# Graph-network kernel: the third mean pass scans in PSUM, and counting marks are spread more densely over the sort

## What is computed

```python
def _sage_conv(x, src, dst, Wl, bl, Wr):
    msg = x[src]
    summed = segment_sum(msg, dst, num_segments=N_NODES)
    cnt = segment_sum(ones, dst, num_segments=N_NODES)
    mean = summed / maximum(cnt, 1.0)[:, None]
    return mean @ Wl.T + bl + x @ Wr.T

h = relu(_sage_conv(x, src, dst, Wl0, bl0, Wr0))
h = relu(_sage_conv(h, src, dst, Wl1, bl1, Wr1))
h = _sage_conv(h, src, dst, Wl2, bl2, Wr2)
x = layernorm(x + h)
```

## Time and profile before

| | |
|---|---|
| median of 3 runs | 2670.53 us |
| the profiled execution | 2668.62 us, of which its span, first to last instruction, is 2666.8 us |
| TensorE (PE) busy | 1858.4 us, 70% |
| VectorE (DVE) busy | 1730.9 us, 65% |
| ScalarE (ACT) busy | 1097.3 us, 41% |
| GpSimd (POOL) busy | 1772.3 us, 66% |
| mean granted TensorE clock | 0.852 of full |

### The profile page before, as it was taken

The page is one execution under the profiler, slowest core; times in us unless marked ns, Lnnn a source line. Parts: engine busy times, 40 slices in busy tenths (PEclk is TensorE's granted clock), DMA queues, the critical chain, the costliest instruction groups (busy, mean ns, idle before and its releaser), DMA issues.

```text
span 2666.8 us, 43662 instructions
## 1 busy us (share of the span) xinstructions
PE 1858.4 (70%) x10441; PEld 1326.4 (50%) x10441; DVE 1730.9 (65%) x5671; ACT 1097.3 (41%) x2508; POOL 1772.3 (66%) x1895
## 2 busy tenths in 40 slices
PE   4536666999979999687777764888778888770000
PEld 2425555666656666465555543555555555540000
DVE  7766977677757777665555543798888887881000
ACT  6952110445434444222222222676666666650000
POOL 0045775776637676447777777777777777776776
PEclk6667999999989999788888786899999999995555
DMA  0014665988969988454444522555444454433231
GB/s 19 0 52 112 170 154 139 179 194 187 191 141 176 192 200 187 131 144 120 138 128 139 160 87 85 148 152 156 146 148 144 143 157 138 147 110 103 93 94 50
DMA packets 366725, 356.94 MB, mean 134 GB/s; under 512 B 46535, under 2 KB 288725, under 8 KB 366585
## 3 DMA queue, kind: packets, MB, share of 16 engines
q1 hardware_dynamic: 310136, 246.40, 30.6%
q0 software_dynamic: 56448, 109.10, 21.5%
HBM read 232.83 MB, written 129.11 MB: 136 GB/s over the span
## 4 chain that ended last, share of the span: by engine, by line
PE 33%; POOL 25%; DVE 17%; issue 17%; DMA 5%; ACT 2%; POOLq 1%; DVEq 0%; SPq 0%; ACTq 0%
POOL GX L674 11%; POOL hsrc L674 8%; PE bank L851 8%; PE bank L871 5%; POOL out_dram L728 4%; PE bank L773 4%; PE bank L899 3%; PE bank L891 3%; PE bank L889 3%; DMA GX<-in_x_dram,idx_a 2%; PE bank L855 2%; DVE hsrc L1231 2%; DVE stats L1357 2%; POOL x_prime L728 2%; DVE hsrc L1232 2%
## 5 line engine op out<-in xcount | busy, mean ns | idle before, releaser
L674 POOL DMA_INDIRECT GX<-mean_product,idx_a x392 | 412.4, 1052 | 128.0 <-issue 114.1
L674 POOL DMA_INDIRECT GX<-in_x_dram,idx_a x392 | 377.8, 964 | 118.3 <-issue 111.1
L851 PE MATMUL bank<-h,wt 128*128 128x512 f32 x588 | 316.3, 649 | 0.0
L1045 ACT ACTIVATE logv<-mv,eps 128x4 f32<-128x4 f32 x245 | 72.2, 295 | 545.9 <-DVE mv L1362 545.8
L728 POOL DMA_INDIRECT x_prime<-normed,idx_b x196 | 198.4, 1012 | 95.9 <-issue 91.7
L728 POOL DMA_INDIRECT out_dram<-XN,idx_b x196 | 192.7, 983 | 74.3 <-issue 64.6
L674 POOL DMA_INDIRECT hsrc<-x_prime,idx_d x196 | 189.1, 965 | 59.7 <-issue 59.7
L674 POOL DMA_INDIRECT GX<-in_edge_attr_dram,idx_a x196 | 189.2, 965 | 58.6 <-issue 53.5
L674 POOL DMA_INDIRECT hsrc<-x_prime,idx_c x196 | 186.6, 952 | 59.7 <-issue 59.7
L773 PE MATMUL bank<-ident,GX 128*128 128x128 f32 x588 | 107.2, 313 | 152.8 <-DMA GX<-in_x_dram,idx_a 146.6
L773 PE MATMUL bank<-ident,hsrc 128*128 128x128 f32 x468 | 86.1, 315 | 157.8 <-DMA hsrc<-x_prime,idx_d 58.2
(11 more groups left out here) (231 smaller groups left out, 4658.5 us busy)
## 6 DMA issues: line engine op xcount, KB each, us to landing
mean_product<-prod SPq DMA_DIRECT2D x147, 256.0 KB
hsrc<-mean_product SPq DMA_DIRECT2D x147, 256.0 KB, 4.4
XN<-in_x_dram SPq DMA_DIRECT2D x98, 256.0 KB, 5.9
x_prime<-normed SPq DMA_DIRECT2D x98, 256.0 KB
XN<-x_prime SPq DMA_DIRECT2D x98, 256.0 KB, 4.6
out_dram<-normed SPq DMA_DIRECT2D x98, 256.0 KB
flag<-same_dst_row SPq DMA_DIRECT2D x147, 128.0 KB, 4.7
XN<-low_row SPq DMA_DIRECT2D x98, 128.0 KB
```

The source lines that it names most:

```text
L674: pool.indirect_dma_start(buf[:, c.slot(U), t, :], None, table, bass.IndirectOffsetOnAxis(ap=idx[:, c.slot(U), t:t + 1], axis=0)).then_inc ...
L851: last = pe.matmul(psum[:, :], wt[:, T_R[i], :], before[:, c.slot(2), :], start=True, stop=not dst_phase)
```

## The change

There are two edits. First, in `mean2` (i = 2) ScalarE rectifies bank 5 in place, VectorE scans straight from bank 5, nothing is written to `hsrc`, and TensorE waits before it writes bank 5 not only until ScalarE is through (`m_h`) but also until the scan of the chunk before is (`m_seg`). Second, the counts of marks: 50 for 44 at the start, 14 for 12 behind an even turn, 3 for 2 in the formula behind an odd one.

```diff
-            mark(44)
+            mark(50)
@@
-                mark(12 if turns % 2 == 0 else 2 + turns // 2)
+                mark(14 if turns % 2 == 0 else 3 + turns // 2)
@@ def mean_turn(c):
                     pe.wait_ge(m_h.of(c), m_h.after(c, 1))
+                    if c.phase == "mean2":
+                        pe.wait_ge(m_seg.of(c), m_seg.after(c, 1))
                     psum = bank[5]
@@ def mean_keep(c):
-                    act.activation(h, bank[5][:, :], ACT.Relu, bias=bcol[:, i - 1:i]).then_inc(m_h.of(c), 1)
+                    act.activation(h if i == 1 else bank[5][:, :], bank[5][:, :], ACT.Relu, bias=bcol[:, i - 1:i]).then_inc(m_h.of(c), 1)
@@ def mean_seg(c):
-                    rows = take_cols(hsrc, c.index() * CH, CH)
+                    rows = take_cols(hsrc, c.index() * CH, CH) if c.phase == "mean1" else bank[5][:, :]
```

## The result

The changed kernel takes 2656.05 us (median of 6 runs, 2651.78 to 2658.71), the kernel before 2670.53 (6 runs, 2667.63 to 2672.39): a ratio of 0.9947, 95% interval [0.9934, 0.9959], so 14.5 us or 0.53% faster.

A forecast was written before the change was run, and what follows sets the result against it. ScalarE's marks bound the tail before mean0, POOL's gathers mean0's middle, TensorE the later mean passes. Gain 16.6 us (16.1 plus 0.5), less 0.7 for bank 5, is 15.9: 2654.6 us against 2670.53, range 2651 to 2660.

The forecast's parts named there:

- Cost in the sort: At the start, TensorE waits for ScalarE's marks before turns 9, 11, 13 and the value columns, turned 4.1 us late.
- Gain in the tail: Behind the value turns fewer marks remain, so mean0's first GX turn comes at 192.05, 16.1 us earlier.
- The clock: In mean0's prologue TensorE's higher clock comes sooner: 0.5 us gained, of a possible 1.4.
- POOL: In mean0's gathers, the first stop shrinks from 22.7 to 2.5 us, the second stays 5.2, and 16.1 us passes through.
- a second stop that grows: Sign of a wrong forecast: POOL's second stop in mean0's gathers, expected near 5 us, getting longer.
- rival (b): Mean0's prologue waits for loads of flags and low rows, not TensorE: some 4 us given back, 2658.6; chance 0.03.
- Mean0 as a whole: The gain at the start passes through mean0 to later stages: 16.6 us with the clock.
- Bank 5 at the start: In the third pass, the second turn waits for the first scan and a wake-up: 0.7 us lost, once.
- Bank 5 in the steady state: In the third pass's later chunks, the smallest room is 1.47 us, so the wait for the scan costs nothing.
- Rival (c): In the third pass TensorE waits for turn, rectifier and scan in every chunk: up to 51 us, 2705; chance 0.04.
- The extra wait: In the third pass, the added wait instruction before TensorE's turn into bank 5: 0 us taken, bounds 0 and 2.7.
- The rectifier: In the third pass, ScalarE's rectifier writing into the bank instead of SBUF: -37 to 0 ns.

The follow-up runs named there:

- Run 4: Counts of marks 50, 13 and 3, no bank edit, against the kernel before: 2654.05 us, ratio 0.9930.
- run 1: Only the denser counts of marks (50, 14, 3), no bank edit, against the kernel before: 2654.41 us, ratio 0.9934.
- run 2: Only the scan from bank 5, old counts of marks, against the kernel before: 2671.93 us, ratio 1.0000.
- run 5: The changed kernel measured again with no edit, against the kernel before: 2662.48 us, ratio 0.9941.
- runs 8 and 9: Third pass's flag loads asked for two steps later: in the kernel before, 2696.97 us, ratio 1.0020; with the bank edit alone, 2702.45 us, ratio 1.0038.
- run 7: Counts 50, 13, 3, leftover marks in TensorE's idle time, plus the bank edit, against the kernel before: 2656.45 us, ratio 0.9925.
- runs 3 and 6: Kernel before with leftover marks in TensorE's idle time, no bank edit: first with old counts, 2648.76 us; second with counts 50, 13, 3, 2653.99 us.
- run 10: The changed kernel with eight flag buffers for four and flags asked for three steps earlier, against the kernel before: 2660.38 us, ratio 0.9936.

## Why the prediction was right

The forecast was 2654.6 us and 15.9 us gained; 2656.05 and 14.5 came out. For the profiled execution it was 2652.7; that took 2658.71, 6.0 more, of which 3.9 were lost behind one late flag. Step by step:

- **Cost in the sort.** 4.1 us late; 4.18 measured. By turns: 0.5, 1.0, 1.4 and 1.4 us are added at turns 9, 11, 13 and the value columns, against 0.4, 1.0, 1.4, 1.35. ScalarE's pace and the ring of 8 are all that this stretch needs. The other value columns are then 3.69 us late (185.76), not 4.1.
- **Gain in the tail.** First GX turn at 192.05; 192.09 measured. That close it is by luck: the marks behind the value turns began 0.4 us before the forecast and took 2.86 us for 2.4. Run 4 was expected at 193.2 by the same sum and came at 192.90.
- **The clock.** I took 0.5 us of 1.4; the second stop of POOL ends 17.29 us earlier, 1.24 more than the GX turn. The upper end was the right one in the trace: once the marks no longer come in a trickle, 1.00 is granted from the first GX turn on. The rule that the prediction named, of the Trainium skill, TensorE: Matmul & The Clock Gate, Part 1: The HAM clock gate, would have given 17.5 us for the marks where I had 16.6; run 1 gave 17.2, which tells neither from the other, and the trace agrees with the rule by that 1.00.
- **POOL.** The first stop was to shrink to 2.5 us; it vanished, since at the higher clock the turn that it waits for ended 5.0 us after the first GX turn (197.08) and not 7.9 as before. POOL's third copy then comes 216.24 - 197.26 = 18.98 us earlier, where POOL itself is the limit (beyond 18.6 us, as forecast), but the second release only 17.29 earlier: the difference of some 1.6 us is the growth of the second stop from 5.20 to 6.76 us. I had named a second stop that grows as a sign of being wrong. It came, but as the other side of a first stop that fell away, and not because something else held mean0. The wait for a low row, which was to stay at 1.86 us, is 3.13: rival (b), but 1.3 us of it and not 4.
- **Mean0 as a whole.** 16.6 was to pass through; 16.0 did at the first copy of mean1. The rest of the 17.29 went into a longer wait for the last product's store, 15.60 us against 14.66.
- **Bank 5 at the start.** 0.7 us; 0.68 by the distance from the first turn to the second, 5.94 against 5.26. The wake-up of 0.14 us in my 0.7 had no row; a turn that waits for a scan starts 0.25 us after its end (846.59 against 845.06 + 1.28). The wait is there in the changed kernel and runs 2 and 5 (0.78 and 0.86 us), but the price is less sure than the match: that distance is 5.16 to 5.66 us in the runs without the edit, and 5.67 to 5.94 in those with it (runs 8 and 9 aside).
- **Bank 5 in the steady state, the step that failed.** "The wait is over before it is reached: nothing." That holds in run 2 and in 44 of 46 distances of the changed kernel. But I took the room of 1.47 us from one execution without a late flag, and asked only whether the scan takes longer, not what else it waits for: a 4.42 us stand for a flag is no longer scan, and it uses the room up in the same way. Term: 0 us taken, 3.9 to 6.3 in three traces, some 2 to 3 in the medians, which the intervals do not tell from 0. Part of it is the lower clock behind a wait (1.75 us in the changed kernel and 1.76 in run 7), which the prediction did not price either. Rival (c) had the mechanism, but as a ring that binds in every chunk; behind the second turn it binds in one or two.
- **The rest.** The extra wait 0 of 2.7 us: run 2's 285.51 against 285.50 says 0. The scan 1280 ns in the third pass, 1280 forecast. The rectifier 661 ns into the bank against 687 into `hsrc`, within my -37 to 0.

So the mechanism of the marks was right and carries the forecast. In the sum two misses stand against each other: the marks gave 17.2 where I had 16.6, and the bank took 2 or 3 where I had 0.7; that only 1.4 us are left between forecast and time is in part luck.

Of rule and rival: the sentence of the Trainium skill, PSUM — Partial Sum Buffer, Summary: rules for kernel authors, to evacuate promptly, is borne out here in a small way. The bank that is held through the scan makes the second turn wait 0.8 us and hands on a late flag to TensorE, which stands 1.1 to 2.5 us for flags 2.7 to 4.9 us late; through `hsrc`, flags 3 to 4.3 us late made TensorE stand 0 to 0.2 us.

What stays open: why SP's queue is slow near the tenth chunk of the third pass in so many executions, and in others (before, runs 1, 3 and 4) makes no flag late. The DMA engines are busy to about 1.0 there, but they are that in quiet stretches as well; no run varied it.

## What to carry to other kernels

When work that a slow engine makes one by one (0.7475 us a mark) is spread over another engine's program, count it through with the ring: TensorE's waiting only moves, as run 4 against run 1 shows, until the marks are put where TensorE has nothing else to do (runs 3 and 6, 22.8 and 22.2 us instead of 17.2). Before a copy out of a bank is dropped, list everything that the reader of the bank waits for, DMAs too: the copy was a buffer against those, and its room has to be taken from executions in which they were late.

## What the runs showed of the hardware

- A pause of TensorE of 2.0 us in full work was followed by a granted clock of 0.66 over the next 5 us (1.00 before and after), which cost about as much again, 1.75 us. The same 0.66 stands behind run 7's second pause (2.14 us, in the window 844.5 to 849.5) and behind run 10's of 3.87 (844 to 849). Behind run 7's first pause (2.00 us) and run 5's of 2.54 and 1.14 us 1.00 was granted, so it does not always come.
- SP's queue took 4.88 us over an issue whose usual time is 0.35, at a DMA share of 0.99; one such stall makes all loads behind it late, whichever they are (flags in the changed kernel, rows of x in run 10).
- A scan of 128x512 takes the same from a bank and from SBUF, 1280 and 1284 ns; a rectifier of that size is 26 ns shorter into the bank.
